# Bf16 parts of the Sinkhorn matrices by transposing parts, and the Sinkhorn loop in two groups

## What is computed

```python
def body(_, la):
    la = la - logsumexp(la, axis=-1, keepdims=True)
    la = la - logsumexp(la, axis=-2, keepdims=True)
    return la
log_alpha = jax.lax.fori_loop(0, N_ITERS, body, logits)      # N_ITERS = 20
attn = jnp.exp(log_alpha)
out = jnp.einsum('bhqk,bhkd->bhqd', attn, v)
```

## Time and profile before

| what | value |
|---|---|
| median of 3 runs | 3279.07 us (3278.24 to 3283.2) |
| profiled execution | 3278.18 us |
| its span | 3276.5 us |
| first stage | 2571.1 to 2640.5 us |
| Sinkhorn loop | 2642.6 to 2846.4 us |

### The profile page before, as it was taken

The page is one execution under the profiler, slowest core; times in us unless marked ns, Lnnn a source line. Parts: engine busy times, 40 slices in busy tenths (PEclk is TensorE's granted clock), DMA queues, the critical chain, the costliest instruction groups (busy, mean ns, idle before and its releaser), DMA issues. The chain is left out here.

```text
span 3276.5 us, 62814 instructions
## 1 busy us (share of the span) xinstructions
PE 3059.1 (93%) x25686; PEld 2669.1 (81%) x25686; DVE 1755.3 (54%) x3257; ACT 1453.0 (44%) x2994; POOL 116.3 (4%) x87
## 2 busy tenths in 40 slices
PE   6899999999999999999999999999889679869997
PEld 5688888888888888888888888888746579859997
DVE  5355655565565556556565555665533788740001
ACT  3355555555555555555555555555522510011111
POOL 0000000000000000000000000000040310100001
PEclk9899999999999999999999999999999655579998
DMA  7311221121121112112112211211350000217761
GB/s 308 115 45 39 75 64 45 49 83 38 47 79 56 39 58 75 39 51 75 58 45 62 65 44 44 80 40 45 97 115 1 16 33 0 82 63 283 251 228 60
DMA packets 234821, 253.16 MB, mean 77 GB/s; under 512 B 22328, under 2 KB 169944, under 8 KB 234096
## 3 DMA queue, kind: packets, MB, share of 16 engines
q1 hardware_dynamic: 233040, 241.79, 23.2%
q0 software_dynamic: 1280, 4.20, 0.4%
q10 hardware_dynamic: 288, 4.19, 0.3%
HBM read 215.42 MB, written 34.70 MB: 76 GB/s over the span
## 5 line engine op out<-in xcount | busy, mean ns | idle before, releaser
L272 PE MATMUL fills<-wv_group,ctxT_hi 128*128 128x256 f32 x4096 | 775.9, 285 | 1.3 <-DVE ctxT_lo L477 0.6
L280 PE MATMUL fills<-ctxT_hi,wk_pairs 128*128 128x512 f32 x2048 | 703.8, 405 | 0.6 <-DVE keys L492 0.6
L272 PEld LDWEIGHTS fills<-wv_group,ctxT_hi 128*128 128x128 f32 x4096 | 643.6, 189 | 23.9 <-issue 20.3
L492 DVE SCALAR_TENSOR_TENSOR keys<-fills,bk,keys 64x512 fp32r<-64x512 f32 x512 | 383.9, 750 | 407.2 <-ACT keys L409 403.6
L272 PE MATMUL fills<-wv_group,ctxT_lo 128*128 128x256 f32 x2048 | 571.4, 279 | 0.0
L409 ACT ACTIVATE keys<-fills,bk 64x512 fp32r<-64x512 f32 x512 | 349.9, 683 | 403.6 <-PE fills L280 400.4
L280 PEld LDWEIGHTS fills<-ctxT_hi,wk_pairs 128*128 128x128 f32 x2048 | 385.7, 188 | 102.6 <-issue 23.8
L280 PE MATMUL fills<-ctxT_lo,wk_pairs 128*128 128x512 f32 x1024 | 401.2, 392 | 0.0
L485 DVE TENSOR_TENSOR values<-fills,values 128x512 fp32r<-128x512 f32 x256 | 176.7, 690 | 415.0 <-ACT values L404 415.0
L272 PEld LDWEIGHTS fills<-wv_group,ctxT_lo 128*128 128x128 f32 x2048 | 386.4, 189 | 0.0
L529 DVE TENSOR_TENSOR probsT<-probsT_ps,probsT 128x512 fp32r<-128x512 f32 x504 | 348.4, 691 | 67.3 <-ACT probsT L441 58.7
(11 more groups left out here) (211 smaller groups left out, 3091.0 us busy)
## 6 DMA issues: line engine op xcount, KB each, us to landing
e_w<-in_L_ffn_W SPq DMA_DIRECT2D x64, 1024.0 KB, 8.8
ctx_stage<-in_ctx SPq DMA_DIRECT2D x128, 256.0 KB, 2.9
wv_group<-wv_split SPq DMA_DIRECT2D x64, 512.0 KB, 4.6
wk_pairs<-wk_split SPq DMA_DIRECT2D x128, 256.0 KB, 3.2
q<-q_split SPq DMA_DIRECT2D x256, 64.0 KB, 2.7
q_split<-p_qb SPq DMA_DIRECT2D x16, 512.0 KB, 3.7
o_parts<-o_half SPq DMA_DIRECT2D x128, 64.0 KB, 1.8
a_ua<-o_parts SPq DMA_DIRECT2D x32, 256.0 KB, 5.4
```

The source lines that it names most:

```text
L272: last = nc.tensor.matmul(pJ[:, bank[0], 256 * k:256 * k + 256], c[:, t, s:s + P], wv[:, w, t, :], start=t + n == 0, stop=t == DT - 1 and ...
L280: last = nc.tensor.matmul(pJ[:, bank[0], :], wk[:, p, w, t, :], c[:, t, 512 * j:512 * j + 512], start=t + n == 0, stop=t == DT - 1 and n == 2)
L492: last = nc.vector.scalar_tensor_tensor(out=keys[lo_rows(j), x, 512 * j:512 * j + 512], in0=pJ[DK * a:DK * a + DK, bk_, :], scalar=bk_sb[h ...
```

## The change

The parts of A are no longer worked out from A. A transpose moves numbers without changing them, so the three parts of A are the transposes of the three parts of A^T. `turn_back` now waits for the third part of A^T and makes twelve bf16 transposes per quad, against a bf16 copy of the identity (`ident_b`): the first parts into `pA`, the second and third into `pA2`. ScalarE copies the first (`a_copy`), VectorE the other two in one copy of 128x1024. The works `a_first`, `a_second`, `a_remainder` and `a_third` and the tile `rest_a` are gone. Lags change: turn_back 4, ScalarE's copy 4, VectorE's copy 5, t_second 1. All steps of all engines are written out. The Sinkhorn loop has two groups of 32 matrices instead of four of 16.

```diff
-                rest_a = sb("c_rest_a", [P, 2, 4, P], F32, s4)
+                ident_b = sb("c_ident", [P, P], BF16, s4)
...
-                pA = ps("c_pA", [P, 2, 4, P], F32, s4)
+                pA = ps("c_pA", [P, 2, 8, P], BF16, s4)
+                pA2 = ps("c_pA2", [P, 2, 2, 4, P], BF16, s4)
...
-                    each_step(pool, (rows, 0), (t_third, 3))
+                    each_step((rows, 0), (t_third, 3))
...
                     def turn_back(n, buf, reused):
-                        pe.wait_ge(exped, n + 1)
+                        pe.wait_ge(t_part3, n + 1)
                         if reused:
+                            pe.wait_ge(a_first, n - 1)
                             pe.wait_ge(a_rest, n - 1)
-                        for k in range(4):
-                            last = nc.tensor.transpose(pA[:, buf, k, :], AT[:, 4 * n + k, :], ident[:, :])
+                        for part in range(3):
+                            for k in range(4):
+                                last = nc.tensor.transpose(pA2[:, buf, part - 1, k, :] if part else pA[:, buf, k, :], at_p[:, part, 4 * n + k, :], ident_b[:, :])
                         last.then_inc(a_turned, 1)
-                    each_step(pe, (turn, 0), (turn_back, 1), looped=False)
+                    pe.wait_ge(made, 1)
+                    each_step((turn, 0), (turn_back, 4))
...
-                    def a_second(n, buf, reused):
-                        act.wait_ge(a_rest, n + 1)
-                        nc.scalar.copy(a_p[:, 1, four(n), :], rest_a[:, buf, :, :]).then_inc(a_part2, 1)
-
-                    def a_first(n, buf, reused):
+                    def a_copy(n, buf, reused):
                         act.wait_ge(a_turned, n + 1)
-                        nc.scalar.copy(a_p[:, 0, four(n), :], pA[:, buf, :, :]).then_inc(a_part1, 1)
-                    each_step(act, (exp, 0), (a_second, 3), (a_first, 1), (t_first, 0))
+                        nc.scalar.copy(a_p[:, 0, four(n), :], pA[:, buf, 0:4, :]).then_inc(a_first, 1)
+                    each_step((exp, 0), (t_first, 0), (a_copy, 4))
...
-                    def a_remainder(n, buf, reused):
...
-                    def a_third(n, buf, reused):
...
-                    each_step(dve, (maxima, 0), (a_third, 4), (a_remainder, 2), (t_second, 2))
+                    def a_copy(n, buf, reused):
+                        dve.wait_ge(a_turned, n + 1)
+                        nc.vector.tensor_copy(a_p[:, 1:3, four(n), :], pA2[:, buf, :, :, :]).then_inc(a_rest, 1)
+                    nc.vector.tensor_copy(ident_b[:, :], ident[:, :]).then_inc(made, 1)
+                    each_step((maxima, 0), (t_second, 1), (a_copy, 5))
             with ExitStack() as s5:
-                NG, GM = 4, NM // 4
-                pV = ps("c_pV", [P, 4, 512], F32, s5)
+                NG, GM = 2, NM // 2
+                pV = ps("c_pV", [P, NG, 512], F32, s5)
```

More of the change, by code:

```diff
@@ L1137, in self_attention, with each_step @@
                 rest_t = sb("c_rest_t", [P, 2, 4, P], F32, s4)
-                rest_a = sb("c_rest_a", [P, 2, 4, P], F32, s4)
+                ident_b = sb("c_ident", [P, P], BF16, s4)
                 nm2 = sb("c_nm2", [P, NM], F32, s4)
                 pLT = ps("c_pLT", [P, 2, 4, P], F32, s4)
-                pA = ps("c_pA", [P, 2, 4, P], F32, s4)
+                pA = ps("c_pA", [P, 2, 8, P], BF16, s4)
+                pA2 = ps("c_pA2", [P, 2, 2, 4, P], BF16, s4)
                 normed, turned, maxed, exped = (sem(n) for n in ("c_normed", "c_turned", "c_maxed", "c_exped"))
                 t_part1, t_rest, t_part2, t_part3 = (sem(n) for n in ("c_t_part1", "c_t_rest", "c_t_part2", "c_t_part3"))
-                a_turned, a_part1, a_rest, a_part2, a_part3 = (sem(n) for n in (
-                    "c_a_turned", "c_a_part1", "c_a_rest", "c_a_part2", "c_a_part3"))
+                made, a_turned, a_first, a_rest = (sem(n) for n in ("c_made", "c_a_turned", "c_a_first", "c_a_rest"))
                 block = s4.enter_context(nc.Block())
-                def each_step(eng, *works, looped=True):
-                    def step(n):
+                def each_step(*works):
+                    for n in range(NQ + 6):
                         for work, lag in works:
@@ L1155, in step @@
                                 work(n - lag, (n - lag) % 2, n - lag >= 2)
[L1156 to L1167, removed]
                 @block.sync
@@ L1244, in t_second @@
                         nc.vector.tensor_copy(at_p[:, 1, four(n), :], rest_t[:, buf, :, :]).then_inc(t_part2, 1)
-                    def a_remainder(n, buf, reused):
[L1247 to L1251, removed]
-                    def a_third(n, buf, reused):
-                        dve.wait_ge(a_part2, n + 1)
-                        nc.vector.tensor_tensor(a_p[:, 2, four(n), :], rest_a[:, buf, :, :], a_p[:, 1, four(n), :],
-                                                ALU.subtract).then_inc(a_part3, 1)
-                    each_step(dve, (maxima, 0), (a_third, 4), (a_remainder, 2), (t_second, 2))
+                    def a_copy(n, buf, reused):
[3 more added lines that the diff above has]
+                    each_step((maxima, 0), (t_second, 1), (a_copy, 5))
             with ExitStack() as s5:
-                NG, GM = 4, NM // 4
-                pV = ps("c_pV", [P, 4, 512], F32, s5)
+                NG, GM = 2, NM // 2
+                pV = ps("c_pV", [P, NG, 512], F32, s5)
                 zero = sb("c_zero", [P, D], F32, s5)
```

## The result

The changed kernel took 3263.54 us (median of 5 runs, 3259.59 to 3265.68) against 3283.2 for the kernel before (5 runs beside it); the ratio is 0.9939 with a 95% interval of 0.9927 to 0.9950. Run a second time (e10) it took 3259.53 against 3278.49, ratio 0.9947 (0.9933 to 0.9961). So it is faster by some 0.5 to 0.6%; 3262.1 was forecast. The profiled execution took 3259.59 us, 18.6 less than the profiled one of before, with a span of 3257.8.

The account below looks back on a forecast made before the run. VectorE-GpSimd turns were taken to bound the first stage, VectorE narrowly over TensorE the Sinkhorn loop. First stage -9.9 and Sinkhorn -6.2 gave -16.1 us, 3278.2 to 3262.1 us; range 3252 to 3271.

Parts of the forecast that it names:

- The first stage's mechanism: Stage forming the bf16 parts: VectorE and GpSimd operations taking turns set the step; the stage gains 9.9 us.
- The sum of 3.28: First stage: four turns of 1.02, 1.15, 0.68 and 0.43 us make the step's period, 3.28 us.
- The tail: From the first stage's last maxima to its end: 10.4 us instead of 11.4, 1.0 less.
- The bounded prices: First stage, per step: twelve bf16 transposes 1.5 us (upper end 3.3), VectorE's PSUM copy 0.69 (upper end 1.22).
- Nothing for writing the stage out: First stage: removing three engines' loops changes nothing since turns set the pace; bounded by 2.0 us either way.
- The wait for t_third: First stage: turn_back's wait on GpSimd costs nothing in steady state; without cover, up to 1.5 us per step.
- Sinkhorn: Sinkhorn loop in two groups: iterations 10.28 instead of 10.52 us, 1.7 behind the last product instead of 3.6; 6.2 less.
- VectorE was the slower by a little: Sinkhorn loop before the change: VectorE needs 10.57 us per iteration, TensorE alone 10.28.
- (a): First stage: VectorE's PSUM copy takes 1.22 us, 3.9 us more, whole 3266; chance 0.27.
- (b): First stage: period stays near 4 us as turns grow; only tail and Sinkhorn gain, whole 3271; chance 0.11.
- (c): First stage, TensorE: bf16 transposes cost as much as fp32, 0.28 us each, whole 3284; chance 0.06.
- (d): Sinkhorn loop: TensorE's clock goes to its upper level, loop 78 us less, whole 3190; chance 0.03.

Follow-up runs that it names:

- e10: The changed kernel itself, unchanged, run a second time: 3259.53 us against 3278.49 for the kernel before, ratio 0.9947.
- e4: Changed kernel with VectorE's 128x1024 copy moved between its subtraction and its rounding of the same step: first stage 54.62 us against 54.68, step 2.96 us.
- e9: Changed kernel with two products per Sinkhorn matrix and third parts not made at all (eight transposes, 512-column copy): first stage 47.64 us, ratio 0.9746 against before.
- e5: Changed kernel with steps 6 to 15 of GpSimd, ScalarE and VectorE in a hardware loop again: first stage 56.26 us against 54.68.
- e2: Kernel before with two Sinkhorn groups and nothing else changed: loop 197.45 us against 203.81, ratio 0.9976 against before.
- e8: Changed kernel with two instead of three products per Sinkhorn matrix, in four groups of 16: loop 201.72 us, iteration 10.41 us.
- e1: Changed kernel with four Sinkhorn groups as before, so its first stage alone: loop 201.48 us against 197.22, ratio 0.9936 against before.
- e11: Changed kernel with four Sinkhorn groups, run again beside the changed kernel: loop 201.76 us against 197.22, ratio 0.9948 against before.
- e6: Changed kernel with every bf16 transpose made twice, 24 per step: first stage 54.83 us against 54.68.

## Why the prediction was right, and where it was off

**The whole.** 3262.1 was forecast, 3263.5 and 3259.5 came. But the two stages gained 21.3 us (14.7 + 6.6), not 16.1. In the profiled execution 2.1 of it is lost ahead of the stages, where nothing was changed (the first stage starts at 2573.21 instead of 2571.14), and 0.5 behind them. In that of e10, the same kernel, the stage starts at 2570.91, 0.2 earlier than before, and 2.3 are lost behind the loop. So the times outside the two stages move by some 2 us between executions, and that the whole came so near is in part luck.

**The first stage's mechanism held, its step was mis-sized.** The turns of VectorE and GpSimd set a step of 2.96 (e4, and the steps ahead of the first copy), and without one of them it fell to 2.56 (e9). That VectorE's list, 2.4 without hold-ups in the prediction, comes to 2.98 with one, level with the turns, wasn't foreseen. The sum of 3.28 took the four durations; three of the turns hold the other engine for less than their duration, and by the ends they are 0.56, 0.90, 0.29 and, with L1169's start behind the rounding, 1.23: 2.98. From step 1 to step 15 that made 41.9 instead of the 45.9 forecast, 4.0 of the missing 4.8 us of this stage. The earlier trace rows had it: L1255 ended 0.55 behind GpSimd's L1184, and I added 0.68 for such a subtraction.

**The tail.** 10.4 was forecast, 9.5 came. The 36 transposes took 4.00 (4.5), at a granted clock of 0.50 (2623.10 to 2627.20), and the way to the last rounding 4.1 (4.4).

**The bounded prices.** Twelve transposes cost 4.00 / 3 = 1.33 at 0.50; 1.5 was taken, 3.3 was the upper end. The copy takes 0.68; 0.69 was taken, 1.22 was the upper end. The Trainium skill's rule on PSUM operands (VectorE: DVE Perf Modes, "Why PSUM operands drop a tier") holds for this bf16 copy: 1024 columns in the 0.68 that 512 fp32 columns take.

**Nothing for writing the stage out.** That was wrong in its reason and inside its bound of 2.0: e5 gives 1.6 us, by its rows from a turn of GpSimd that starts 0.2 later in a loop.

**The wait for t_third.** Its cover held: in the steady state TensorE's transposes wait for VectorE's copy (0.69 in the step shown), not for GpSimd.

**Sinkhorn.** An iteration of 10.26 (10.28 forecast), 1.7 behind the last product (1.7), the loop 6.6 less (6.2). That VectorE was the slower by a little is what e2 and e8 show. Not foreseen: four groups alone would have gained 2.0 to 2.3 us behind the new stage (e1, e11), so the groups' own share in the final kernel is 4.3 to 4.5.

**The rivals.** (a) is out by the copy's row (its sum took 0.59 for what L1255 lost, which is 0.56 in the earlier trace rows; that is 0.4 us of its 3.9), (b) by the step, (c) by the transposes' price and, with twice the work, by the clock (e6). (d) didn't happen: the loop stayed at 0.50. Its price was wrong as well: by e6's one stretch products of this shape would gain 1.7 of their 26.7 ns, 7296 of them an estimated 12 us, not 78. The Trainium skill gives a floor of about 25 ns from start to start, however few the columns (TensorE: Matmul & The Clock Gate, "Wait — 56ns, not 53.3ns?"); e6 agrees with 25.0.

## What to carry to other kernels

An engine that is busy 99% of a stage need not set its pace: count what each engine needs per round, the pause at a loop's head too, and look at which of them runs late when the stage ends. Where two engines hold each other up, a turn's price is the distance between the ends of consecutive turns, not its duration. Here moving work into one of the waits only moved the wait (e4), and taking a turn away shortened the round (e9, where other work went too). An instruction of such a chain that takes no longer than undisturbed is a sign that a second limit lies as near as the first. When a small part of a long kernel changes, measure it by its own first and last row: whole times can agree for a reason that lies elsewhere.

## What wasn't expected of the hardware

Products of three columns with a load each follow each other by 26.7 ns at the lower clock and, over 1.8 us of e6, by 25.0 at the upper. The same VectorE loop pauses 0.33 us at its head in the kernel before and 0.20 in e1, e8 and e11. With the stage in hardware loops (e5) GpSimd took a turn 0.2 us later than written out.
